# A fused attention and FFN block on one core: another order of projections, row selection, normalisation and output products

## The reference

```python
xn  = (x - mean(x)) / sqrt(var(x) + 1e-5)
# attention: 16 heads of 64
a   = xn * rsqrt(mean(xn**2) + eps) * norm_w
q, k, v = split(a @ Wq), split(a @ Wkv)
q   = q / |q| * (q_gamma + 1) * 8;  k = k / |k| * (k_gamma + 1) * 8
p   = softmax(tanh(q k^T / 50) * 50 / 8)
att = (p @ v) @ Wo
# FFN: both weights get a per-batch low-rank part made of 16 token rows
lt  = xn[:, 1:17];  even, odd = lt[:, ::2], lt[:, 1::2]
m1  = even[:, :4, :, None] * odd[:, :4, None, :]     # reshaped to 512 x 128
m2  = even[:, 4:, :, None] * odd[:, 4:, None, :]     # reshaped to 128 x 512
h   = gelu(xn @ (W1 + scale*m1)^T + b1)
out = x + att + h @ (W2 + scale*m2)^T + b2
```

## Time and profile before

| | |
|---|---|
| median of three runs | 1260.57 us |
| the profiled execution, and its span | 1261.8 us, 1259.8 us |
| TensorE (PE) matmuls busy, weight loads (PEld) | 1165.6 us (93%), 972.3 us (77%) |
| ScalarE (ACT) busy | 1082.2 us (86%) |
| VectorE (DVE) busy | 1032.2 us (82%) |
| GpSimd (POOL) busy | 917.6 us (73%) |
| mean granted TensorE clock | 0.992 of full |
| DMA queues that carry data, share of 16 engines | 4.7% |

### The profile page before, as it was taken

The page is one execution under the profiler, slowest core; times in us unless marked ns, Lnnn a source line. Parts: engine busy times, 40 slices in busy tenths (PEclk is TensorE's granted clock), DMA queues, the critical chain, the costliest instruction groups (busy, mean ns, idle before and its releaser), DMA issues.

```text
span 1259.8 us, 36165 instructions
## 1 busy us (share of the span) xinstructions
PE 1165.6 (93%) x13897; PEld 972.3 (77%) x13897; DVE 1032.2 (82%) x2153; ACT 1082.2 (86%) x2055; POOL 917.6 (73%) x1105
## 2 busy tenths in 40 slices
PE   3789999999999999999999999999999999999988
PEld 2468887778877778878778878778878778878777
DVE  6788889888889888889888889888889888888862
ACT  3589898889898889888888988888988888988885
POOL 4477777777777777877777877777777777777663
PEclk9899999999999999999999999999999999999999
DMA  4000000000000000000000000000000000000000
GB/s 132 10 11 11 14 16 7 15 15 11 15 15 7 15 15 11 15 15 7 15 15 11 14 16 7 15 15 11 14 15 7 15 15 15 10 11 11 11 6 9
DMA packets 32224, 19.41 MB, mean 15 GB/s; under 512 B 3508, under 2 KB 31288, under 8 KB 32056
## 3 DMA queue, kind: packets, MB, share of 16 engines
q1 hardware_dynamic: 32056, 17.12, 4.7%
HBM read 12.13 MB, written 4.19 MB: 13 GB/s over the span
## 4 chain that ended last, share of the span: by engine, by line
PE 42%; DVE 25%; ACT 19%; issue 11%; POOL 1%; ACTq 0%; POOLq 0%
PE ps_scores L481 8%; ACT probs L563 6%; PE ps_aux L455 5%; DVE qk L729 4%; PE ps_aux L448 4%; PE ps_aux L406 4%; PE ps_y L525 4%; DVE heads_T L738 3%; DVE sel_rows L760 3%; DVE qk L694 3%; PE ps_aux L408 3%; PE ps_aux L407 3%; ACT L596 3%; DVE norm L667 3%; ACT hid L596 3%
## 5 line engine op out<-in xcount | busy, mean ns | idle before, releaser
L905 POOL TENSOR_TENSOR probs_lo<-probs 128x512 f16<-128x512 f32 x512 | 586.3, 1150 | 235.1 <-ACT probs L563 232.9
L555 ACT ACTIVATE clamped<-ps_scores 128x512 f32<-128x512 f32 x512 | 310.3, 606 | 124.5 <-PE ps_scores L481 124.4
L563 ACT ACTIVATE probs<-clamped 128x512 f32<-128x512 f32 x512 | 324.9, 635 | 0.4
L503 PE MATMUL ps_o<-v_hi,probs 128*128 128x65 bf16 x2048 | 240.0, 195 | 4.5 <-DVE o_sb L706 2.7
L504 PE MATMUL ps_o<-v_lo,probs 128*128 128x64 bf16 x2048 | 239.2, 193 | 0.0
L505 PE MATMUL ps_o<-v_hi,probs_lo 128*128 128x65 bf16 x2048 | 238.9, 194 | 0.0
L481 PE MATMUL ps_scores<-heads_T 64*128 64x256 f16 x3072 | 212.9, 271 | 14.2 <-ACT clamped L555 14.0
L406 PE MATMUL ps_aux<-w_hi,xhT_hi 128*128 128x512 f32 x384 | 191.5, 499 | 31.9 <-DVE qk L729 21.6
L503 PEld LDWEIGHTS ps_o<-v_hi,probs 128*128 128x128 bf16 x2048 | 192.1, 99 | 30.1 <-issue 18.2
L504 PEld LDWEIGHTS ps_o<-v_lo,probs 128*128 128x128 bf16 x2048 | 189.8, 99 | 5.0
L505 PEld LDWEIGHTS ps_o<-v_hi,probs_lo 128*128 128x128 f16 x2048 | 190.2, 98 | 0.0
(11 more groups left out here) (83 smaller groups left out, 2211.2 us busy)
## 6 DMA issues: line engine op xcount, KB each, us to landing
x_in<-in_L_attn_tokens_dram SPq DMA_DIRECT2D x32, 128.0 KB, 2.3
x_res<-in_L_attn_tokens_dram SPq DMA_DIRECT2D x32, 128.0 KB, 2.3
out_dram<-y_sb SPq DMA_DIRECT2D x32, 128.0 KB, 1.9
sel_raw<-xn SPq DMA_DIRECT2D x192, 4.0 KB
qk<-in_L_attn_Wkv_dram SPq DMA_DIRECT2D x2, 512.0 KB, 5.4
qk<-in_L_attn_Wq_dram SPq DMA_DIRECT2D x1, 512.0 KB, 3.6
qk<-in_L_ffn_W_dram SPq DMA_DIRECT2D x2, 256.0 KB
hid<-in_L_attn_q_gamma_dram SPq DMA_DIRECT2D x1, 512.0 KB, 7.0
```

Source lines behind the costliest of these rows:

```text
L503: pe.matmul(full, hi[:, col], v_hi[:, par, u, h], start=(u == 0), stop=False)
L555: nc.scalar.activation(clamped[:, buf], ps_scores[:, s % SCORE_BANKS], ACT.Tanh).then_inc(clamp_done, 1)
L563: nc.scalar.activation(probs[:, buf], clamped[:, buf], ACT.Exp, bias=LIFT, scale=SOFTCLAMP * DH ** -0.5).then_inc(probs_done, 1)
L905: g.tensor_tensor(probs_lo[:, buf], probs[:, buf], probs[:, buf].bitcast(BF16)[:, 1::2], ALU.subtract).then_inc(lo_made, 1)
```

## The change

The same instructions are issued, in other orders. `AUX` pairs projections in one slot (q3 with k2, v2 with v3, q0 with q1, and both transposes qkT2 and qkT3 behind them); other tasks move by up to two slots, and with them who shares a bank with whom. `select` is cut in two: choosing the rows moves from slot 14 of the step before to slot 0, the masked copies to slot 2, for the batch in the attention stage. Layer norm's statistics move from slot 1 to 3, POOL's power from 1 to 6 and its bias sum from 4 to 10. The first `normalise` stands ahead of the effective W2 in slot 10, the second ahead of the splits in slot 12. The output products stand in seven slots instead of twelve.

```diff
 AUX = [
     (1, "k", 0, 1), (1, "k", 1, 1), (1, "q", 2, 1),
     (2, "qkT", 4, 0), (2, "qkT", 5, 0),
-    (3, "q", 3, 1),
-    (4, "oT", 0, -1), (4, "oT", 1, -1), (4, "k", 2, 1),
-    (5, "k", 3, 1), (5, "low", 0, 0), (5, "v", 0, 1),
-    (6, "oT", 2, -1), (6, "v", 1, 1),
+    (3, "q", 3, 1), (3, "k", 2, 1),
+    (4, "k", 3, 1), (4, "oT", 0, -1),
+    (5, "oT", 1, -1), (5, "low", 0, 0),
+    (6, "oT", 2, -1), (6, "v", 0, 1),
     (7, "oT", 3, -1), (7, "qkT", 6, 0),
-    (8, "qkT", 7, 0), (8, "v", 2, 1),
+    (8, "qkT", 7, 0), (8, "v", 1, 1),
     (9, "hid", 0, 0), (9, "hid", 1, 0),
-    (10, "low", 1, 0), (10, "v", 3, 1),
-    (11, "xhT", 0, 2),
+    (10, "low", 1, 0),
+    (11, "v", 2, 1), (11, "v", 3, 1), (11, "xhT", 0, 2),
     (12, "qkT", 0, 1), (12, "qkT", 1, 1),
     (13, "xnT", 0, 2),
-    (14, "q", 0, 2), (14, "qkT", 2, 1),
-    (15, "qkT", 3, 1), (15, "q", 1, 2),
+    (14, "q", 0, 2), (14, "q", 1, 2),
+    (15, "qkT", 2, 1), (15, "qkT", 3, 1),
 ]
...
 VECTOR_STEPS = [
-    [("result",), ("sum", 0)],
-    [("norm_stats",), ("sum", 1), ("divide",), ("splits",)],
...
+    [("result",), ("sum", 0), ("select_rows",)],
+    [("sum", 1), ("divide",), ("splits",)],
+    [("splits",), ("select_low",)],
+    [("divide",), ("splits",), ("sum", 2), ("norm_stats",)],
...
-    [("updates",), ("splits",), ("normalise", 0, 1)],
-    [("splits",), ("divide",), ("normalise", 1, 1)],
-    [("splits",)],
+    [("normalise", 0, 1), ("updates",)],
+    [("splits",), ("divide",)],
+    [("normalise", 1, 1), ("splits",)],
...
-Y_PRODUCTS = {3: 2, 5: 1, 6: 1, 7: 2, 8: 1, 9: 5, 10: 5, 11: 1, 12: 3, 13: 1, 14: 1, 15: 1}
+Y_PRODUCTS = {5: 4, 7: 2, 9: 3, 10: 6, 12: 2, 13: 5, 15: 2}
```

More of the change, by code:

```diff
@@ L79 @@
 VECTOR_STEPS = [
-    [("result",), ("sum", 0)],
-    [("norm_stats",), ("sum", 1), ("divide",), ("splits",)],
-    [("splits",)],
-    [("divide",), ("sum", 2), ("splits",)],
+    [("result",), ("sum", 0), ("select_rows",)],
+    [("sum", 1), ("divide",), ("splits",)],
+    [("splits",), ("select_low",)],
+    [("divide",), ("splits",), ("sum", 2), ("norm_stats",)],
     [("sum", 3), ("sum", 4), ("normalise", 3, 0)],
-    [("divide",), ("updates",), ("sum", 5), ("splits",)],
-    [("sum", 6), ("splits",)],
-    [("sum", 7), ("seed",), ("divide",), ("splits",)],
+    [("divide",), ("updates",), ("sum", 5)],
+    [("sum", 6), ("splits",), ("sum", 7)],
+    [("seed",), ("divide",), ("splits",)],
     [("splits",)],
     [("divide",), ("norm_apply",)],
-    [("updates",), ("splits",), ("normalise", 0, 1)],
-    [("splits",), ("divide",), ("normalise", 1, 1)],
+    [("normalise", 0, 1), ("updates",)],
+    [("splits",), ("divide",)],
+    [("normalise", 1, 1), ("splits",)],
+    [("divide",), ("normalise", 2, 1)],
     [("splits",)],
-    [("divide",), ("normalise", 2, 1)],
-    [("splits",), ("select",)],
     [("splits",), ("divide",)],
@@ L98 @@
     [("lo",)],
-    [("lo",), ("rstd",)],
+    [("lo",)],
     [("lo",), ("square", 0)],
     [("lo",), ("square", 1)],
-    [("lo",), ("bias",)],
     [("lo",), ("square", 2)],
     [("lo",), ("square", 3)],
+    [("lo",), ("rstd",)],
     [("lo",), ("newton", 0)],
@@ L107 @@
     [("lo",), ("newton", 2)],
-    [("lo",)],
+    [("lo",), ("bias",)],
     [("lo",)],
@@ L748, in aux, with select_rows @@
                         .then_inc(weff_made, 1)
-            def select(st):
-                b, _, _ = st.batch(1)
+            def select_rows(st):
+                b, _, _ = st.batch(0)
                 dve.wait_ge(rows_loaded, 16 * 6 * (b + 1))
@@ L761, in select, with select_low @@
                         .then_inc(sel_copied, 1)
+            def select_low(st):
+                b, _, _ = st.batch(0)
                 dve.wait_ge(sel_copied, 3 * b + 3)
@@ L797, in run @@
                             result(st)
-                        elif what == "select" and "front" in st.stages:
-                            select(st)
+                        elif what == "select_rows" and "attn" in st.stages:
+                            select_rows(st)
+                        elif what == "select_low" and "attn" in st.stages:
+                            select_low(st)
                         elif what == "sum" and "front" in st.stages:
```

## The result

The changed kernel takes 1277.09 us (median of four runs, 1275.91 to 1278.12), the kernel before 1261.09 us beside it: a ratio of 1.0123, 95% interval 1.0105 to 1.0141. It is slower by 16 us; the forecast was 1222 us, faster.

A forecast was written before the change was run, and what follows sets the result against it. TensorE was taken as fullest, with 35.3 us of work in a 37.69 us step. Gains of 0.1 and 1.6 less 0.37, taken as 1.25 a step, gave 39 us off: 1222 us, range 1210 to 1236.

The forecast's parts named there:

- the five gaps: TensorE's waits in slots 1, 3, 12 (two) and 15 of the kernel before, 2.4 us of a 37.69 us step.
- the wait at k1: Slot 1: k1 waits 0.42 us for qkT3's bank, held by VectorE; forecast to go.
- the wait of slot 12's scores for the tanh: Slot 12: scores start 0.41 us over their price, waiting for head 11's tanh; forecast to go.
- Slots 8 to 12: The normalise's wait goes, a wait for the v splits takes its place; a gain of only 0.1 us a step.
- Slots 12 to 15: Three more products, q1 behind q0, q1's wait gone: a cost of 0.37 us a step.
- the slack at qkT3: Slot 15: q0 scaled at 460.3, TensorE wants its bank at 460.6; 0.3 us, the thinnest slack of the step.
- rival 3: Slots 12 to 15: both multiplications take 2.03 us under GpSimd's low parts, qkT3 waits 1.3; 1271 us, chance 0.08.
- Slots 0 to 7: v1 moved out, k1's wait gone, q3's wait cut from 0.73 to 0.2: a gain of 1.6 us a step.
- rows 0.3 and 1.33: Slots 0 to 7: lengths taken for VectorE's row choice, in the sum that has q2 scaled by S+6.05.
- signs of failure: Forecast fails if q0 is scaled too late for qkT3, row choice exceeds 1.6 us, or v2's copy starts over 0.55 late.
- The rule that was weighed: Shared port: VectorE tensor_tensor with two SBUF inputs and GpSimd reading SBUF lock each other out; multiplication 1.22 or 2.03 us.
- The rest: GpSimd's power and bias sum, head 10's low part, row choice's loaded rows and SyncE's loads: said to cost nothing.

The follow-up runs named there:

- run 6: Changed kernel with GpSimd's low parts of the probabilities and squares of k cut to 8 of 512 columns: 1228.17 us, ratio 0.9732.
- run 11: Kernel before with only GpSimd's new order (power in slot 6, bias sum in slot 10, last two squares a slot earlier): 1279.39 us, ratio 1.013.
- run 12: Changed kernel with only the output products back in their old slots: 1283.79 us, ratio 1.017.
- run 8: Changed kernel with GpSimd's low parts and squares cut to 8 columns and the selection whole in slot 14 of the step before: 1229.73 us, ratio 0.9737.
- run 16: Changed kernel, products in old slots, w2_eff ahead of first normalise, rows in slot 14, masked copies in slot 15 ahead of the divide: 1303.84 us, ratio 1.0321.

## Why the prediction was wrong

It forecast 1222 us; measured 1277. Step by step:

- *What bounds the kernel, and the five gaps.* Right in the main: the wait at k1 and the wait of slot 12's scores for the tanh went, as forecast. TensorE's work, the step less its waits read from the starts, is about 35.6 us in the changed kernel and in run 6, a little over the 35.3 that the prediction took.
- *Slots 8 to 12.* Right. The normalise waited 1.40 us for the inverse norm, then 1.23 went by before v's copy was ready, and the transposes of slot 12 were released by the v split, 1.20 us after their scores began (forecast 1.30). 10.34 us against 10.24.
- *Slots 12 to 15.* The slack at qkT3 that was called the thinnest did go, but not by rival 3's cause. One of its two multiplications was hit (1.86 us, the other 1.21), and still VectorE was idle before it scaled q0, waiting for ScalarE's square of q0 (the row stands below). The transposes of slot 15 took 1.09 us instead of 0.93. They took 1.10 in run 6 too, where no multiplication was hit and this idle time was 0.80. So the 0.16 us are ScalarE's, a term that the prediction did not have, and the collision here cost nothing.

```profile
429.43 1.29 DVE L729 TENSOR_TENSOR qk<-ps_aux,g_bc 128x512 f32<-128x512 f32 x2 [0.15 <-ACT sq_q L575]
```

- *Slots 0 to 7.* This step failed: the prediction priced the moved selection by lengths that did not hold in its new place. It gave q3 a wait of 0.2, and oT0 and oT3 0.1 together with 0.6 as the upper bound; they were 0.67, 0.77 and 0.54, so 1.3 for the two. TensorE reached q3 at S+5.85, as forecast, but q2 was scaled at S+6.47 and not at S+6.05. The "rows 0.3 and 1.33" came from their old neighbourhood, and the cast took 0.64; row choice took 2.03 us against 1.6, one of the signs of failure that the prediction named. The two masked copies stand in it with no row and no length. Its 0.1 us at oT0 and oT3 fits their lengths without company: in run 6 they took 0.93 us until the next instruction and neither bank was late; in the changed kernel they took 1.96. Run 6 shows the step of the sum to be right in all else: with GpSimd quiet the same slots take 16.83 us against 16.7 forecast.
- *The rule that was weighed.* It was the rule that decides, and it was applied at one place only. The rows of two lengths for one instruction were taken as a rival's risk in slots 12 to 15, when the change moves the selection to just where GpSimd has its squares and low parts: each instruction with inputs in SBUF had to be checked against GpSimd's list at its new time. Rival 3's price for a step, 1.6 us over the forecast (1.25 and 0.35), was near the 1.7 lost in slots 0 to 8; its place was not, and it cost nothing at its own place, so its 1271 us comes near the measured 1277 by luck.
- *The rest.* "These cost nothing" was checked for GpSimd's own lateness, not for what the bias sum and the power do to VectorE's multiplications. In the kernel before they cost 16 us, with the two squares (run 11). In the changed kernel the first multiplication of slot 10 is over before the bias sum (419.34 against 422.02), and slots 8 to 12 took what was forecast, so there nothing shows a cost.

What stays open: how the parts add up. Four that cost 107 us singly cost 16 together with VectorE's new order, which no run tried by itself, and the products change sign with the selection. Each changes when VectorE and GpSimd meet, and no run here separates that for the task order.

## What to carry to other kernels

A move of instructions keeps their durations only if the other engine's company stays the same. Before a reordering is priced, mark the instructions whose lengths differ between places in the trace (here 1.22 and 2.03 us for one multiplication), find what ran on the other engine in the long cases, and lay that engine's list beside the new order. And test a part by taking the other engine's long instructions away, in both kernels: that told here that the orders were good (1239 to 1228 us) and that the collisions had eaten them. A part that is slower alone can still be worth having, and the reverse.

## What the runs showed of the hardware

- The block goes both ways. In the changed kernel a square of k that takes 1.04 us took 2.02 at 445.76, and ended 0.90 after the multiplication that was under way (446.88). GpSimd's squares rose from 1039 to 1370 ns on average, while the bias sum fell from 1595 to 726 ns in slot 10.
- Very small instructions are hit as hard as large ones: var_eps, 128x2 elements, took 941 ns on average in run 12 against 169 in run 8, and the selection's 8x128 differences 634 in the changed kernel against 282 in run 6.
- VectorE's reads from PSUM with one SBUF input (the splits, the scalings) and its reductions of 128x512 elements kept means of 672 to 689 ns in every run, whatever GpSimd did. These are the ones that can stand beside GpSimd's long instructions.
- TensorE's granted clock can turn a wait into a second loss. In run 16 it fell to 0.50 for some 3 us after a wait of 2.05 us, in about every second step, and twelve score matmuls and eight transposes took 1.12 and 1.76 us from start to start instead of 0.76 and 0.93.
